# The causal mask of self-attention's diagonal blocks: a GpSimd select behind the exponential, or a TensorE product in front of it

## The chip, the cores and the metric

The kernel runs on one core of a Trainium2 chip. The metric is the device time of one launch in microseconds, lower is better. A core has five engines that run their own instruction streams and wait for one another by semaphores: TensorE (PE in the profile; its weight loads are listed apart as PEld), VectorE (DVE), ScalarE (ACT), GpSimd (POOL) and SyncE (SP), which here only issues DMAs.

## The reference, cut to what matters

One decoder layer: self-attention, cross-attention and a mixture of experts, each with a residual and a layer norm. The change touches self-attention alone, for 2 batches of 2048 tokens, 512 channels, 16 heads of 32:

```python
q = (x @ Wq.T + bq).reshape(B, T, H, D); k = ...; v = ...
scores = jnp.einsum('bqhd,bkhd->bhqk', q, k) * attn_scale[0]
masked = (qb >= kb) & (idx[None, :] - idx[:, None] - 2 * (kb - qb) >= 1)   # qb, kb: starts of 64-token chunks
scores = jnp.where(masked[None, None], -jnp.inf, scores)
attn = jax.nn.softmax(scores, axis=-1)
out = jnp.einsum('bhqk,bkhd->bqhd', attn, v).reshape(B, T, C)
return out @ Wo.T + bo
```

With i and j the places of key and query in their chunks of 64, this masks all keys of earlier chunks, in the query's own chunk those with i > j, and none of later chunks. The kernel computes the blocks of keys from a query's own block of 128 to the end of the sequence. In a diagonal block of 128 keys by 128 queries, the keys of the first chunk are masked for all queries of the second, the keys of the second chunk for none of the first, and within a chunk the keys that come after their query.

## The kernel before, in words

`self_attention` goes over 8 **groups** (2 batches, 4 groups of 4 heads). In a group the 2048 queries are cut into 4 chunks c of 512 (chunk 0 is the last 512 queries), and the keys into blocks of 128. A **round** is one chunk with one key block: `round_at` lists 40 rounds of a group, 4, 8, 12 and 16 for c = 0, 1, 2, 3; k numbers the rounds within a chunk, from the last key block down. The last four rounds of every chunk are those where the key block meets the chunk's own queries. There only `width` columns are left (512, 384, 256, 128 in the four), and the last 128 of them are the diagonal block. So 16 of 40 rounds are **diagonal rounds**. Two rounds make a **pair**, numbered 0 to 19 here; the diagonal pairs are 0 and 1 (c = 0), 4 and 5 (c = 1), 10 and 11 (c = 2), 18 and 19 (c = 3), the first of each two with 512 and 384 columns, the second with 256 and 128.

For one head of a round:

- TensorE writes the scores, 128 keys by `width` queries, into one of three PSUM banks `sbank` (L440). The rows of `kparts` and `qparts` carry high and low parts and the negated row maximum, so that a score comes out with its maximum already taken off. In a diagonal round a second product (L443), the bf16 identity `identb` by the bf16 `maskT`, adds -1e30 on the masked places, in the same bank.
- ScalarE takes the exponential from the bank into `probs` (L548), a ring of four rounds. `exp_done` tells of it; TensorE waits for the exponential of three heads before when it writes the next score.
- One pair later TensorE multiplies `probs` with the values (L458, `weighted`) and with ones for the denominator (L469). For the latter GpSimd first adds the pair's two rounds of `probs` into `both` (`add_pair`: a copy at L331 where the even round is wider, then the sum at L334), which takes 128 x 2048 elements in a full pair.

Around the scores, in the same TensorE stream, lie the **maxima segments** (L406): score products of a later chunk, on which VectorE takes row maxima (L607 with `maskS`, L611 without), through three banks `wbank`; the projections of keys, queries and values for a later chunk (L382, L389), whose results ScalarE (L513) and VectorE (L579, L591) take out and SP spreads over partitions by 12 DMAs a chunk (L227); and four transposes (L413) that bring the maxima into `qparts`, which ScalarE copies (L521). `maxima_in` and `others_in` say in which round each of them stands. In a pair's last round four segments are held back and stand between the products of `weighted`. At the start of a group's c = 0, VectorE also copies the last chunk's denominator (L645) and takes its reciprocal (L650), GpSimd multiplies (`multiply`, L344), and SP stores (L234) before it goes on to the next 12 spreading DMAs.

The order on every engine is the order of the code. TensorE's is: scores of pair p with their segments, then `weighted` of pair p - 1. ScalarE may start the exponentials of pair p when the products with pair p - 2 have read `probs` and GpSimd's sum of pair p - 2 is done.

## Time and profile before

| | |
|---|---|
| runs | 3275.59, 3286.88, 3287.71 us; median 3286.88 |
| the profiled execution | 3281.05 us, its span 3279.3 us |
| busy over the span | PE 2963.8 us (90%), DVE 2039.8 (62%), ACT 1453.1 (44%), POOL 1520.5 (46%) |
| self-attention | from 58 us (first score) to 1699 us, some 208 us for each of 8 groups |
| L443, the mask's product | 512 times in the program: 16 rounds x 4 heads x 8 groups |
| mean granted clock of TensorE | 0.961 of full |

The page lists, for each engine and line, how often a group of instructions ran, how long one took, and how long the engine was idle before it and on whom it waited. The timeline lists instructions with start and duration; like ones in a row are merged. Matmuls are pipelined: each is shown from its start to a modelled end, so how much of the engine one takes is read from the distance between two starts, and not from its duration.

### The profile page before, as it was taken

To read this page: it belongs to the slowest core of one execution; us is meant where nothing else is said; L and a number is where in the kernel's file an instruction comes from. 1 tells how busy PE (TensorE), PEld (TensorE's weight loads), DVE (VectorE), ACT (ScalarE), POOL (GpSimd) and SP (SyncE) were. 2 spreads that over 40 slices of the span, in tenths; PEclk is the share of its full clock that TensorE was granted. 3 is DMA by queue.
4 is the path that set the end of the run, shared out by engine and by line. 5 is a ranking of instruction groups with operands and counts; after the bars stand their busy time and mean duration, and the time that the engine had idled before them with its cause. 6 is when DMAs were issued, how large, how long until landed. Compare 5 with 4: busy or idle time off the path is not lost. (4 is left out here: it accounts for less than half of the span.)

```text
span 3279.3 us, 59175 instructions
## 1 busy us (share of the span) xinstructions
PE 2963.8 (90%) x19197; PEld 1934.0 (59%) x19197; DVE 2039.8 (62%) x4795; ACT 1453.1 (44%) x3375; POOL 1520.5 (46%) x1093
## 2 busy tenths in 40 slices
PE   7998999989989999898988979999799994999992
PEld 4444444444444444444434468888688883888882
DVE  4645646556465574554725568888477774777776
ACT  1443544434444444444442257777322222555551
POOL 3343443424434344243452234444377774665656
PEclk8999999999999999999999989999999996999996
DMA  4223022221221212212207522222222224999997
GB/s 114 62 64 82 7 74 79 58 63 32 75 78 44 66 44 74 78 31 67 66 30 253 189 84 88 79 82 84 84 71 68 68 61 140 258 254 259 257 254 265
DMA packets 185030, 343.33 MB, mean 105 GB/s; under 512 B 36136, under 2 KB 54696, under 8 KB 183848
## 3 DMA queue, kind: packets, MB, share of 16 engines
q1 hardware_dynamic: 135336, 250.90, 25.7%
q0 software_dynamic: 28800, 48.43, 6.8%
q10 hardware_dynamic: 20736, 41.95, 3.3%
q8 instruction: 92, 1.51, 0.2%
q14 instruction: 66, 0.54, 0.1%
HBM read 206.96 MB, written 83.89 MB: 89 GB/s over the span
## 5 line engine op out<-in xcount | busy, mean ns | idle before, releaser
L548 ACT ACTIVATE sa_probs<-sa_s 128x512 f32<-128x512 f32 (+3 forms) x1280 | 609.8, 540 | 692.9 <-PE sa_s L440 353.1
L334 POOL TENSOR_TENSOR sa_both<-sa_probs 128x2048 f32<-128x2048 f32 (+2 forms) x160 | 590.0, 3687 | 628.4 <-ACT sa_probs L548 616.9
L406 PE MATMUL sa_w<-sa_parts 96*128 96x512 f32 (+3 forms) x1280 | 515.0, 440 | 81.7 <-DVE sa_pmax L607 43.2
L440 PE MATMUL sa_s<-sa_parts 128*128 128x512 f32 (+3 forms) x1280 | 480.4, 409 | 27.3 <-ACT sa_probs L548 21.4
L607 DVE CUSTOM_DVE_ANT_0 sa_w<-sa_w,sa_maskS 128x512 f32<-128x512 f32 (+3 forms) x512 | 327.5, 649 | 238.7 <-PE sa_w L406 234.2
L406 PEld LDWEIGHTS sa_w<-sa_parts 96*128 96x128 f32 x1280 | 232.3, 195 | 409.4 <-issue 202.5
L611 DVE TENSOR_REDUCE sa_pmax<-sa_w 128x1 f32<-128x512 f32 (+3 forms) x768 | 422.7, 585 | 47.1 <-PE sa_w L406 44.0
L440 PEld LDWEIGHTS sa_s<-sa_parts 128*128 128x128 f32 x1280 | 242.0, 193 | 168.1 <-ACT sa_probs L548 96.6
L1519 POOL DMA_INDIRECT token_and_weight_of_slot<-rt_entry,rt_sl x256 | 261.0, 1020 | 124.4 <-issue 91.3
L458 PE MATMUL sa_pv<-sa_probs,sa_values 128*32 128x512 f32 (+3 forms) x2560 | 284.2, 538 | 0.0
L1252 ACT ACTIVATE xa_sm<-xa_sm,xa_nmax 128x154 f32<-128x154 f32 x512 | 209.4, 414 | 54.9 <-DVE xa_nmax L1175 54.9
L1831 POOL DMA_INDIRECT scratch_residual<-ex_y,ex_target x90 | 162.1, 1801 | 140.8 <-DMA scratch_residual<-ex_y,ex_target 109.2
L331 POOL COPY sa_both<-sa_probs 128x512 f32<-128x512 f32 x64 | 39.1, 611 | 342.7 <-ACT sa_probs L548 333.3
L1011 POOL TENSOR_TENSOR xa_pmain<-xa_sm,xa_rrec 128x2048 f32<-128x2048 f32 x32 | 115.9, 3622 | 109.8 <-DVE xa_rrec L1179 109.8
L469 PE MATMUL sa_pv<-sa_both,sa_ones 128*32 128x512 f32 (+1 forms) x1280 | 155.0, 556 | 0.0
L1893 PE MATMUL ex_yps<-ex_w2h,ex_hTh 128*128 128x512 f32 x540 | 148.1, 412 | 4.6 <-ACT ex_hTh L1926 4.3
L1876 PE MATMUL ex_h<-ex_xeT,ex_w1h 128*128 128x256 f32 x1080 | 145.4, 284 | 2.4 <-ACT ex_w1h L1905 2.4
L1041 PE MATMUL xa_qps<-cross_xT,cross_wq 128*128 128x128 f32 x1024 | 128.9, 281 | 20.4 <-DMA cross_xT<-scratch_x_T 16.2
L1876 PE MATMUL ex_h<-ex_xeT,ex_w3h 128*128 128x256 f32 x1080 | 145.3, 283 | 0.0
L1876 PEld LDWEIGHTS ex_h<-ex_xeT,ex_w1h 128*128 128x128 f32 x1080 | 139.7, 190 | 6.7 <-issue 2.8
L1876 PEld LDWEIGHTS ex_h<-ex_xeT,ex_w3h 128*128 128x128 f32 x1080 | 136.8, 190 | 0.0
L1041 PEld LDWEIGHTS xa_qps<-cross_xT,cross_wq 128*128 128x128 f32 x1024 | 123.1, 197 | 21.3 <-issue 21.3
(236 smaller groups left out, 5360.0 us busy)
## 6 DMA issues: line engine op xcount, KB each, us to landing
list_w<-in_w SPq DMA_DIRECT2D x138, 512.0 KB, 5.6
sa_parts<-early_halves SPq DMA_DIRECT2D x384, 128.0 KB, 2.4
early_xt<-in_xT SPq DMA_DIRECT2D x32, 1024.0 KB, 5.7
scratch_attention_T<-sa_oT SPq DMA_DIRECT2D x32, 256.0 KB, 2.4
on_at<-scratch_attention_T SPq DMA_DIRECT2D x32, 256.0 KB, 3.1
on_xr<-in_x SPq DMA_DIRECT2D x32, 256.0 KB, 3.4
scratch_x<-on_xn ACTq DMA_DIRECT2D x32, 256.0 KB, 2.1
scratch_x_T<-on_xnT ACTq DMA_DIRECT2D x32, 256.0 KB, 3.4
```

The source lines that it names most:

```text
L334: pool.tensor_tensor(both[:, p % 2, :, 0:w], probs[:, even, :, 0:w], probs[:, odd, :, 0:w], ALU.add).then_inc(both_ready, 1)
L406: nc.tensor.matmul(ps[:, 0:w], qparts[0:3 * HD, h, q0:q0 + P], kparts[0:3 * HD, h, k0:k0 + w], start=True, stop=True).then_inc(work_ready, 1)
L440: mm = nc.tensor.matmul(ps[:, 0:w], kparts[:, h, kb * P:(kb + 1) * P], qparts[:, h, q0:q0 + w], start=True, stop=not diag)
L458: mm = nc.tensor.matmul(pvbank[0][a:a + HD, 0:w], values[:, kb, h, :], probs[:, r % NPB, h, 0:w], start=kb == NKB - 1, stop=kb == QB * chu ...
L548: nc.scalar.activation(probs[:, r % NPB, h, 0:w], sbank[n % NSB][:, 0:w], ACT.Exp).then_inc(exp_done, 1)
L607: dve.tensor_tensor_reduce(out=wbank[b][:, 0:width_], in0=wbank[b][:, 0:width_], in1=maskS[:, 0:width_], scale=1.0, scalar=LOWEST, op0=ALU ...
L611: dve.tensor_reduce(pmax[:, j * GH + h, s:s + 1], wbank[b][:, 0:width_], AX.X, ALU.max).then_inc(work_free[b], 1)
L1041: mm = nc.tensor.matmul(qps[:, g * P:(g + 1) * P], wq[:, k, g * P:(g + 1) * P], xT[:, s, k], start=k == 0, stop=k == KT - 1)
L1252: nc.scalar.activation(sm[:, s, h], sm[:, s, h], ACT.Exp, bias=nmax[:, s, h:h + 1], accum_out=rsum[:, s, h:h + 1]).then_inc(exp_done, 1)
L1519: pool.indirect_dma_start(out=table, out_offset=bass.IndirectOffsetOnAxis(ap=sl[:, s, k:k + 1], axis=0), in_=entry[:, s, k], in_offset=Non ...
L1831: pool.indirect_dma_start(out=res, out_offset=bass.IndirectOffsetOnAxis(ap=target[:, s, j:j + 1], axis=0), in_=y[:, s, j], in_offset=None, ...
L1876: mm = nc.tensor.matmul(bank[f][:, 0:UNIT], wt[:, s, a, k, f * P:(f + 1) * P], xeT[:, s, b, k], start=k == 0 and n == 0, stop=k == KT - 1 ...
```

## The change

In diagonal rounds the product L443 is gone, with `identb` and `maskT`. The exponential is taken of unmasked scores. Behind it GpSimd runs `mask_round` in `add_pair`, before the copy and the sum of the pair: two selects in place on `probs` that write zero on masked places, the first on partitions 0 to 63 with 4 heads x 128 columns, the second on partitions 64 to 127 with 4 heads x 64 columns, each waited for by the next. `weighted` waits for the new semaphore `masked` in diagonal rounds, in place of `exp_done`. In the preparation on GpSimd three memsets and three selects fall away. `maskS` and the maxima stay.

```diff
+    diagonal = [r for r, (c, k) in enumerate(round_at) if kbs(c)[k] < QB * (chunk_q(c) + 1)]
+    NDIAG = len(diagonal)
+    MPARTS = 2
...
-            for t in (identb, identf, maskS, maskT, mcol):
+            for t in (identf, maskS, mcol):
                 step(pool.memset(t[:], 0.0))
...
+            def mask_round(it, r):
+                c, k = round_at[r]
+                w = width(c, kbs(c)[k])
+                pool.wait_ge(exp_done, it * NU + (NSB + GH * (r + 1)))
+                apart(pool, passed)
+                H = P // 2
+                done = (it * NDIAG + diagonal.index(r)) * MPARTS
+                pool.wait_ge(both_ready, it * NPAIR + (r // 2 + 2))
+                first = probs[0:H, r % NPB, :, w - P:w]
+                pool.affine_select(out=first, in_=first, compare_op=ALU.is_ge, fill=0.0, base=0,
+                                   pattern=[[0, GH], [-H, 2], [1, H]], channel_multiplier=-1).then_inc(masked, 1)
+                pool.wait_ge(masked, done + 1)
+                second = probs[H:P, r % NPB, :, w - H:w]
+                pool.affine_select(out=second, in_=second, compare_op=ALU.is_ge, fill=0.0, base=0,
+                                   pattern=[[0, GH], [1, H]], channel_multiplier=-1).then_inc(masked, 1)
+                pool.wait_ge(masked, done + 2)
+
             def add_pair(it, p):
                 even, odd = 2 * p % NPB, (2 * p + 1) % NPB
+                for r in (2 * p, 2 * p + 1):
+                    if r in diagonal:
+                        mask_round(it, r)
...
-                diag = kb < QB * (chunk_q(c) + 1)
                 mm = nc.tensor.matmul(ps[:, 0:w], kparts[:, h, kb * P:(kb + 1) * P], qparts[:, h, q0:q0 + w],
-                                      start=True, stop=not diag)
-                if diag:
-                    mm = nc.tensor.matmul(ps[:, w - P:w], identb[:], maskT[:], start=False, stop=True)
+                                      start=True, stop=True)
                 mm.then_inc(s_ready, 1)
...
-                    pe.wait_ge(exp_done, it * NU + (NSB + GH * r + GH))
+                    if r in diagonal:
+                        pe.wait_ge(masked, (it * NDIAG + (diagonal.index(r) + 1)) * MPARTS)
+                    else:
+                        pe.wait_ge(exp_done, it * NU + (NSB + GH * r + GH))
```

On TensorE, in the scores of pair 4 (c = 1, round of 512 columns going over into the round of 384), before. `sa_work_free` is VectorE's release of a bank of segments, `sa_exp_done` ScalarE's exponential:

```order
L406 MATMUL sa_w<-sa_parts 128x512 [waits sa_work_free2]
L440 MATMUL sa_s<-sa_parts 128x512 [waits sa_exp_done]
L443 MATMUL sa_s<-sa_maskT,sa_identb 128x128
L406 MATMUL sa_w<-sa_parts 128x512 [waits sa_work_free0]
L440 MATMUL sa_s<-sa_parts 128x384 [waits sa_exp_done]
L443 MATMUL sa_s<-sa_maskT,sa_identb 128x128
L406 MATMUL sa_w<-sa_parts 128x128 [waits sa_work_free1]
```

The same place in the changed kernel, where L425 is the segment's line and L458 the score's:

```order
L425 MATMUL sa_w<-sa_parts 128x512 [waits sa_work_free2]
L458 MATMUL sa_s<-sa_parts 128x512 [waits sa_exp_done]
L425 MATMUL sa_w<-sa_parts 128x512 [waits sa_work_free0]
L458 MATMUL sa_s<-sa_parts 128x384 [waits sa_exp_done]
L425 MATMUL sa_w<-sa_parts 128x128 [waits sa_work_free1]
```

The product between a score and the next segment or score is gone, nothing else moved there.

On GpSimd, the sum of pair 9 and the two diagonal pairs 10 and 11 (c = 2), before:

```order
L334 TENSOR_TENSOR sa_both<-sa_probs 128x2048 [waits sa_ones_done,sa_exp_done] x4
L331 COPY sa_both<-sa_probs 128x4x128 [waits sa_ones_done,sa_exp_done]
L334 TENSOR_TENSOR sa_both<-sa_probs 128x4x384 [waits sa_rest_copied]
L331 COPY sa_both<-sa_probs 128x4x128 [waits sa_ones_done,sa_exp_done]
L334 TENSOR_TENSOR sa_both<-sa_probs 128x4x128 [waits sa_rest_copied]
```

And in the changed kernel, from the same sum to the end of pair 10 (L350 is the copy, L353 the sum):

```order
L353 TENSOR_TENSOR sa_both<-sa_probs 128x2048 [waits sa_ones_done,sa_exp_done] x4
L330 AFFINE_SELECT sa_probs<-sa_probs 64x4x128 [waits sa_exp_done,sa_both_ready]
L334 AFFINE_SELECT sa_probs<-sa_probs 64x4x64 [waits sa_masked]
L330 AFFINE_SELECT sa_probs<-sa_probs 64x4x128 [waits sa_masked,sa_exp_done,sa_both_ready]
L334 AFFINE_SELECT sa_probs<-sa_probs 64x4x64 [waits sa_masked]
L350 COPY sa_both<-sa_probs 128x4x128 [waits sa_exp_done,sa_masked,sa_ones_done]
L353 TENSOR_TENSOR sa_both<-sa_probs 128x4x384 [waits sa_rest_copied]
```

Four selects stand ahead of the copy and the sum of a diagonal pair; the first two wait for the even round's exponentials alone.

On TensorE, `weighted` of pair 4 behind the scores of pair 5, before:

```order
L458 MATMUL sa_pv<-sa_probs,sa_values 32x512 [waits sa_exp_done]
L458 MATMUL sa_pv<-sa_probs,sa_values 32x512 x3
L458 MATMUL sa_pv<-sa_probs,sa_values 32x384 [waits sa_exp_done]
L458 MATMUL sa_pv<-sa_probs,sa_values 32x384 x3
L469 MATMUL sa_pv<-sa_both,sa_ones 32x512 [waits sa_both_ready]
```

And in the changed kernel (L477 the products with the values, L488 those with ones):

```order
L477 MATMUL sa_pv<-sa_probs,sa_values 32x512 [waits sa_masked]
L477 MATMUL sa_pv<-sa_probs,sa_values 32x512 x3
L477 MATMUL sa_pv<-sa_probs,sa_values 32x384 [waits sa_masked]
L477 MATMUL sa_pv<-sa_probs,sa_values 32x384 x3
L488 MATMUL sa_pv<-sa_both,sa_ones 32x512 [waits sa_both_ready]
```

The products stand where they stood, and wait for GpSimd's selects where they waited for ScalarE.

## Rows read from the trace of the kernel before

**Rows 1.** Busy time by window (PE, PEld, DVE, ACT, POOL, granted clock), one group.

```profile
400.00:607.00 207.00, 192.67 (x1064) 96.05 (x1063) 118.05 (x262) 91.91 (x187) 83.64 (x32) 0.97 0.22 61
```

**Rows 2.** Line L443: count, ns min/median/max, first and last start.

```profile
L443 PE MATMUL sa_s<-sa_maskT,sa_identb x512: 229/230/330, 58.7 to 1695.0; 128*128 128x128 bf16 x171
```

**Rows 3.** TensorE's timeline (start, duration in us), a round without a mask.

```profile
437.84 0.34 PE L406 MATMUL sa_w<-sa_parts 96*128 96x384 f32 x1
438.01 0.39 PE L440 MATMUL sa_s<-sa_parts 128*128 128x512 f32 x1
438.25 0.34 PE L406 MATMUL sa_w<-sa_parts 96*128 96x384 f32 x1
```

**Rows 4.** TensorE's timeline, diagonal pair 18.

```profile
456.02 0.48 PE L406 MATMUL sa_w<-sa_parts 96*128 96x512 f32 x1
456.34 0.40 PE L440 MATMUL sa_s<-sa_parts 128*128 128x512 f32 x1
456.58 0.23 PE L443 MATMUL sa_s<-sa_maskT,sa_identb 128*128 128x128 bf16 x1
456.62 0.48 PE L406 MATMUL sa_w<-sa_parts 96*128 96x512 f32 x1
```

**Rows 5.** ScalarE's timeline: exponentials of pairs 18 and 11, then of an unmasked round.

```profile
456.33 3.84 ACT L548 ACTIVATE sa_probs<-sa_s 128x512 f32<-128x512 f32 x8 [0.68 <-PE sa_s L443]
...
600.31 2.27 ACT L548 ACTIVATE sa_probs<-sa_s 128x256 f32<-128x256 f32 x8 [4.12 <-PE sa_s L443]
...
445.74 2.06 ACT L548 ACTIVATE sa_probs<-sa_s 128x512 f32<-128x512 f32 x4 [3.60 <-PE sa_s L440]
```

**Rows 6.** Groups by form, 200 to 1600 us: busy us, mean ns | idle before.

```profile
L548 ACT ACTIVATE sa_probs<-sa_s 128x384 f32<-128x384 f32 x108 | 48.0, 493 | 10.8 <-PE sa_s L443 10.4
L548 ACT ACTIVATE sa_probs<-sa_s 128x256 f32<-128x256 f32 x108 | 38.3, 384 | 127.6 <-PE sa_s L443 94.8 <-POOL sa_both L334 31.3
L548 ACT ACTIVATE sa_probs<-sa_s 128x128 f32<-128x128 f32 x108 | 25.0, 277 | 39.5 <-PE sa_s L443 37.4
```

**Rows 7.** VectorE by window, the scores of pair 4.

```profile
538.20:545.20 7.00, 6.86 (x19) 1.00 0.38 131
```

**Rows 8.** Timeline across pairs 1 and 2: GpSimd, SP's queue, TensorE.

```profile
701.17 1.27 POOL L344 TENSOR_TENSOR sa_oT<-sa_raw,sa_rden 128x512 f32<-128x512 f32 x1 [4.55 <-DVE sa_rden L650]
...
703.06 7.68 SPq L227 DMA_DIRECT2D sa_parts<-early_halves  x12
...
713.12 0.73 PE L406 MATMUL sa_w<-sa_parts 96*128 96x512 f32 x2
```

**Rows 9.** GpSimd's timeline while it prepares, the selects there are.

```profile
24.86 0.29 POOL L305 TENSOR_SCALAR_AFFINE_SELECT sa_identf<-sa_identf 128x128 f32<-128x128 f32 x1
...
25.72 0.23 POOL L313 TENSOR_SCALAR_AFFINE_SELECT sa_maskS<-sa_maskS 64x64 f32<-64x64 f32 x1
26.10 0.23 POOL L316 TENSOR_SCALAR_AFFINE_SELECT sa_maskT<-sa_maskT 64x64 bf16<-64x64 bf16 x1
```

**Rows 10.** GpSimd's groups by form: other operations, busy us and mean ns.

```profile
L1488 POOL IOTA rt_spare_row<- 128x256 int32 x1 | 0.4, 357 | 0.1
L334 POOL TENSOR_TENSOR sa_both<-sa_probs 128x2048 f32<-128x2048 f32 x79 | 360.6, 4565 | 532.8 <-ACT sa_probs L548 532.8
L1808 POOL COPY ex_source<-ex_token 128x2 int32 x47 | 34.1, 726 | 14.0 <-issue 8.6 <-PE ex_tps L1862 5.4
```

**Rows 11.** Timelines of GpSimd and TensorE: the sum of pair 4 and its reader.

```profile
546.06 3.46 POOL L334 TENSOR_TENSOR sa_both<-sa_probs 128x1536 f32<-128x1536 f32 x1 [0.18 <-POOL sa_both L331]
...
552.96 1.04 PE L469 MATMUL sa_pv<-sa_both,sa_ones 128*32 128x512 f32 x8
```

**Rows 12.** TensorE's timeline: the values' projection in pair 1, and in pair 16.

```profile
703.52 5.38 PE L389 MATMUL sa_w<-sa_wraw,early_xt 128*128 128x128 f32 x32
...
657.65 3.73 PE L389 MATMUL sa_w<-sa_wraw,early_xt 128*128 128x128 f32 x32
```

**Rows 13.** Busy time by window (columns as in rows 1), pair 1: the granted clock.

```profile
700.50:706.50 6.00, 4.79 (x21) 4.51 (x22) 3.63 (x14) 0.77 (x2) 1.27 (x1) 0.50 0.45 119
```

More of the change, by code:

```diff
@@ L183, in self_attention @@
         shift_ready = sem("shift_ready")
-        s_ready = sem("s_ready"); exp_done = sem("exp_done"); pv_done = sem("pv_done")
+        s_ready = sem("s_ready"); exp_done = sem("exp_done"); masked = sem("masked"); pv_done = sem("pv_done")
         both_ready = sem("both_ready"); rest_copied = sem("rest_copied"); ones_done = sem("ones_done")
@@ L303, in _ @@
             step(pool.memset(kparts[3 * HD:3 * HD + 2].bitcast(F32), 1.0))
-            for t in (identb, identf):
+            for t in (identf,):
                 step(pool.affine_select(out=t[:], in_=t[:], compare_op=ALU.not_equal, fill=1.0, base=0,
@@ L308, in _ @@
             step(pool.memset(maskS[H:P, 0:H], NEG))
-            step(pool.memset(maskT[0:H, H:P], NEG))
             for a in (0, H):
@@ L314, in _ @@
                                         pattern=[[-1, H]], channel_multiplier=1))
-                v = maskT[a:a + H, a:a + H]
-                step(pool.affine_select(out=v, in_=v, compare_op=ALU.is_ge, fill=NEG, base=0,
-                                        pattern=[[1, H]], channel_multiplier=-1))
             pool.sem_inc(consts_set, 1)
             pool.sem_inc(both_ready, 2)
+            def mask_round(it, r):
[14 more added lines that the diff above has]
+                pool.wait_ge(masked, done + 2)
             def add_pair(it, p):
                 even, odd = 2 * p % NPB, (2 * p + 1) % NPB
+                for r in (2 * p, 2 * p + 1):
+                    if r in diagonal:
+                        mask_round(it, r)
                 c, k = round_at[2 * p]
```

2 lines of the change are left out of this document (removed).

## The prediction, made before the changed kernel ran

> **What bounds the kernel now.** I read the busy time of one group of self-attention first. TensorE is busy 192.67 of 207 us, and no other engine comes near: VectorE 118, ScalarE 92, GpSimd 84 [rows 1]. The reader is to see that work taken from TensorE can be worth time here, and that GpSimd has 123 us a group to spare. An average does not tell where the work falls, so next I went through the timeline of one group, pair by pair, and asked of each diagonal pair what its TensorE stream waits for. Only there does the change act.
>
> **What a product costs TensorE.** 512 of them ran [rows 2], 64 a group. The duration of 230 ns is a latency, not a price. Starts tell the price. Without a mask a segment of 384 columns holds the engine 0.17 us (437.84 to 438.01) and a score of 512 columns 0.24 (438.01 to 438.25) [rows 3]; a segment of 512 columns at the same pace would take 0.23, together 0.47. In a diagonal round the segment of 512 takes 0.32 (456.02 to 456.34), the score 0.24, and the product itself 0.04 (456.58 to 456.62), together 0.60 [rows 4]. So a product costs 0.04 of its own and about 0.08 in the instruction behind it, 0.12 us together. If all of this were on the path, the change would give 64 x 0.12 x 8 = 61 us. The Trainium skill (TensorE: Matmul & The Clock Gate, "Back-to-back issue gap") has 81 ns for a matmul of 128 columns in a stream of weight loads and matmuls; by that figure the most would be 41 us. The rows show more, because a short product does not cover the weight load of what follows, and I use the rows.
>
> **What of it is on the path,** pair by pair, in one group:
>
> - Pairs 18, 5 and 11 are bound by ScalarE: their eight exponentials run without a gap, 3.84 us in pair 18 and 2.27 in pair 11, and pair 5 is built like 11 [rows 5]. TensorE can be only three scores ahead. What a faster TensorE can give is what the exponentials' own pace leaves. Four of 512 columns back to back took 2.06 us at about 0.60 each, so they start 0.49 apart, about 0.12 less than one lasts [rows 5]; with the same 0.12 off the durations of the narrower ones [rows 6] the others start 0.37 (384 columns), 0.26 (256) and 0.16 (128) apart. I take 0.19 for the last, since a weight load and a wait stand between. Pair 18: 4 x 0.49 + 3 x 0.37 + 0.49 = 3.56, which is 0.28 less than 3.84. Pair 11: 4 x 0.26 + 3 x 0.19 + 0.28 = 1.89, 0.38 less than 2.27. The first exponential starts about 0.08 sooner, and behind the last score the last product is gone (0.12). That is 0.5 for pair 18 and, rounded down for the ring of three banks, 0.4 each for 5 and 11.
> - Pair 19 (256 and 128 columns) has four segments among its first four scores, and TensorE is the later one there: four products at 0.12, and its last four scores are bound like pair 5's. I take 0.5. Pair 10 (seven segments in its first round) is TensorE's too, but for two products that stand ahead of a wait for VectorE: 0.6. Pair 0 has two projections; of its eight products two stand between the keys' projection and a wait for VectorE's half of it: 0.5.
> - Pair 4 has 16 segments for VectorE, which is busy 6.86 of 7.00 us there [rows 7]. TensorE only waits longer for a bank. I take 0.2, for the last scores.
> - Pair 1 gives nothing. Ahead of pair 2, TensorE's first segment needs keys and queries that come by 12 DMAs. These stand on SP behind the store of the last group's output, which waits for GpSimd's multiplication (701.17 to 702.44), which waited for VectorE's reciprocal. The DMAs are issued from 703.06 to 710.74 and TensorE's segment starts at 713.12 [rows 8]. That chain starts at the end of the last pair's products, in pair 0, and all eight products of pair 1 lie beside it.
>
> The sum is 0.5 + 0.4 + 0.4 + 0.5 + 0.6 + 0.5 + 0.2 = 3.1 us a group, of 7.7 that the products cost, or 24.8 in eight groups. The preparation loses six GpSimd instructions, worth nothing: they run until 27 us, and the first score is at 58 [rows 2, 9].
>
> **What the selects cost GpSimd.** A select of 128 columns took 0.29 us, one of 64 columns 0.23: 0.06 us for 64 elements, so 0.94 ns an element in each partition on top of 0.17 us [rows 9]. Between two that wait for each other lie 0.15 us (25.72 + 0.23 to 26.10) [rows 9]. The new ones have patterns of two and three levels, which no select of the trace has; the nearest row is an iota over 256 elements with several levels, 0.357 us [rows 10], no dearer than 0.17 + 256 x 0.94 ns = 0.41. So 512 elements cost 0.65, 256 elements 0.41, with two gaps M = 1.36 us a round, 16 x 1.36 = 22 us a group on an engine with 123 to spare. From above, M is bounded by other rows: a fixed part of 0.73 as in the copy of two elements, and the sum's 4565 / 2048 = 2.23 ns an element [rows 10], 2 x 0.73 + 768 x 0.00223 + 0.30 = 3.5 us. From below by the two gaps and the two fixed parts, 0.66. I take 1.36, because the nearest row is the same operation.
>
> **Who waits for them.** The new wait stands ahead of `weighted`; behind it on TensorE is queued everything that follows, the next pair's scores first. But `weighted` of a pair runs behind the scores of the next one. The tightest place is the sum: in pair 4 it ends at 549.52, and TensorE's product with ones starts at 552.96 [rows 11], 3.44 us of cover, which shrinks to some 2.9 as pairs 4 and 5 get shorter. The sum now comes later by M, as the even round's selects run beside the odd round's exponentials (4 x 0.37 = 1.5 us). 1.36 fits into 2.9, and pair 10 is alike. Behind pair 0's sum GpSimd's multiplication is next, for which it now sits idle 4.55 us until VectorE's reciprocal is there [rows 8]; a sum that ends 1.36 later does not delay it. At the end of the last group no pair covers the selects: 1.3 us, once.
>
> So 24.8 - 1.3 = 23.5 us: the profiled execution, 3281.05 us around a span of 3279.3, would take 3257.5. It lies 5.8 below the median of the runs shown; against the median the sum says 3263, which I forecast. With the terms that I chose between (0.2 to 0.7 for pair 4, 0 to 0.3 for pair 1, a tenth or two for the others either way) the gain is 15 to 35, the time 3252 to 3272.
>
> **The rivals.**
>
> - **More of the price comes through.** If VectorE and ScalarE give way with TensorE, since they wait for it between pairs, six tenths to all of 61 us are gained: 3226 to 3250. For it speaks that ScalarE is idle 4.12 us ahead of pair 11 [rows 5]; against it, that it has no gap within.
> - **Next to nothing.** TensorE's clock is 0.50 of full over 6 us in pair 1 [rows 13], behind a stretch where it stands still for VectorE, that is 1.2 in place of 2.4 GHz. There the values' projection took 5.38 us; at the full clock, in pair 16, 3.73 [rows 12]. With less work TensorE stands still longer there and in the ScalarE-bound pairs. If each group has one more such stretch, it costs 1.65 x 8 = 13 us, and the gain is 10: 3277. For it speaks that the clock falls in the group already where TensorE idles.
> - **GpSimd becomes late.** If the selects are dear, M above 1.5 delays the sum by 2M - 1.5, and TensorE waits 2M - 1.5 - 2.9 in pairs 4 and 10 each. This eats the 3.1 us a group from M = 3.0 on. At the bound from rows, M = 3.5, it is 8 x (2 x 2.6 - 3.1) = 17 us more than before: 3304. At M = 4.0, 33 more: 3320. Against it speak the selects' rows, 0.94 ns an element where the bound takes 2.23. The Trainium skill (GPSIMD Engine Reference, "Elementwise — side-by-side cycle accounting") has 12 cycles an element for branching that depends on data, which speaks against a select on GpSimd; by this page, as an estimate at its 1.2 GHz, a round would take 8 us and the kernel some 160 us more. The slope of rows 9 is a tenth of it.
> - **The change does not do what it says.** The order of the changed kernel shows no product in the scores and four selects a diagonal pair, so I leave this out.
>
> **How the numbers follow.** My forecast has 0.55, more of the price 0.12, next to nothing 0.23, GpSimd late 0.10. About 0.5% (16 us) is what a measurement here can tell from no change. Faster by more than that is below 3270.5: nearly all of the forecast's case and all of the first rival, 0.63. Slower is above 3303, most of the last case, 0.08. Within, 0.29. The range from 3238 to 3280 leaves out the better part of the first rival's lower end and the last rival, under 2 in 10.
>
> **What the profile of the changed kernel would show.** The price: starts of segment and score 0.47 apart in pair 18's first round, if ScalarE lets them. The exponentials of pair 11 in about 1.9 us, those of pair 18 in 3.5. VectorE still without a gap in pair 4. In pair 1 TensorE waits for the DMAs longer by some 0.5 us. The selects of 512 elements at 0.65 us and of 256 at 0.41, and no TensorE wait that GpSimd ends. I would be wrong if the selects took over 1.5 us a piece, if the granted clock fell in new places, or if groups got shorter by more than 4.5 us.

## The result, and the profile after

The changed kernel takes 3306.99 us in the median of five runs (3300.33 to 3308.62). The kernel before took 3286.88 in the median of the five beside it (3275.59 to 3288.60). The ratio is 1.0068 with a 95% interval of 1.0048 to 1.0088. I had forecast 3263 us and at most 3280. It came out slower.

In the traces, self-attention ends at 1719.5 us, before at 1704.4 (counted to the end of GpSimd's last multiplication), so 15.1 us are lost there. The two profiled executions are 26.0 us apart (spans of 3279.3 and 3305.3), the medians 20.1. The rest lies in stages that the change does not touch: the experts took 490.8 us against 484.1. Over the traces of this study that stage lies between 480 and 491 us with the same code, so I read nothing into it.

The busy time, as line 1 of the page:

```profile
PE 2952.7 (89%) x18685; PEld 1920.8 (58%) x18685; DVE 2068.2 (63%) x4795; ACT 1446.7 (44%) x3375; POOL 1656.9 (50%) x1343
```

TensorE lost 11 us of work, GpSimd took on 136, and **VectorE is 28 us busier, though the change gives it nothing to do**. One group by window (PE, PEld, DVE, ACT, POOL, granted clock), to set beside [rows 1]:

```profile
474.95:684.42 209.47, 191.45 (x1010) 93.79 (x1008) 121.66 (x262) 92.22 (x188) 100.92 (x65) 0.98 0.22 60
```

VectorE has the same 262 instructions and is busy 121.66 us, where it was 118.05. The selects are as forecast, by GpSimd's groups by form, 200 to 1600 us:

```profile
L353 POOL TENSOR_TENSOR sa_both<-sa_probs 128x1536 f32<-128x1536 f32 x26 | 90.0, 3462 | 4.8 <-POOL sa_both L350 4.8
L330 POOL TENSOR_SCALAR_AFFINE_SELECT sa_probs<-sa_probs 64x512 f32<-64x512 f32 x106 | 70.4, 664 | 169.9 <-ACT sa_probs L567 165.4 <-POOL sa_probs L334 3.6
L334 POOL TENSOR_SCALAR_AFFINE_SELECT sa_probs<-sa_probs 64x256 f32<-64x256 f32 x106 | 44.2, 417 | 7.2
```

**Which pairs changed.** I took the start of each pair's first score from the traces. The lengths at the full clock, in us; pairs not shown are the same:

| pair | before | product out, no selects | changed kernel |
|---|---|---|---|
| 0 | 14.46 | 14.20 | 14.20 |
| 4 | 9.48 | 9.37 | 9.37 |
| 5 | 5.73 | 5.53 | **6.66** |
| 10 | 9.01 | 8.54 | 8.55 |
| 11 | 5.40 | 5.19 | **6.32** |
| 18 | 8.42 | 8.04 | 8.04 |
| 19 | 7.10 | 6.95 | 6.95 |

Of these seven, five got shorter with the change and two longer. (Pair 1, which hangs on DMAs, varies between 16.6 and 18.2 us behind the first group in all three.) The engines in pair 5 of the third group, timelines of GpSimd, then VectorE, then TensorE (start, duration, what ended the idle time). L353 is the sum of pair 4 into `both`; L639 to L645 are `row_max`, which brings the row maxima of a chunk into shape for the transposes L432. L641 negates, L644 copies, L645 subtracts, 16 elements a partition each:

```profile
548.80 3.46 POOL L353 TENSOR_TENSOR sa_both<-sa_probs 128x1536 f32<-128x1536 f32 x1 [0.18 <-POOL sa_both L350]
552.33 0.69 POOL L330 TENSOR_SCALAR_AFFINE_SELECT sa_probs<-sa_probs 64x512 f32<-64x512 f32 x1
553.09 0.41 POOL L334 TENSOR_SCALAR_AFFINE_SELECT sa_probs<-sa_probs 64x256 f32<-64x256 f32 x1
```

```profile
550.01 0.20 DVE L639 TENSOR_REDUCE sa_mrow<-sa_pmax 128x16 f32<-128x48 f32 x1
550.25 2.04 DVE L641 TENSOR_SCALAR sa_mhi<-sa_mrow 128x16 fp32r<-128x16 f32 x1
552.32 0.18 DVE L644 COPY sa_mcol<-sa_mhi 128x16 f32<-128x16 f32 x1
552.41 0.65 DVE L645 SCALAR_TENSOR_TENSOR sa_mcol<-sa_mrow,sa_mhi 128x16 f32<-128x16 f32 x1
```

```profile
550.88 1.35 PE L458 MATMUL sa_s<-sa_parts 128*128 128x256 f32 x5 [0.32 <-ACT sa_probs L567]
553.20 0.63 PE L432 MATMUL sa_w<-sa_identf,sa_mcol 128*128 128x128 f32 x4 [0.97 <-DVE sa_mcol L645]
553.76 1.71 PE L477 MATMUL sa_pv<-sa_probs,sa_values 128*32 128x512 f32 x16
```

The negation of 16 elements "lasts" 2.04 us. It ends at 552.29, 0.03 behind the end of GpSimd's sum (552.26), and the subtraction ends at 553.06, 0.04 behind the end of the select. TensorE's transposes stand behind it and start 0.97 us late; all of `weighted`, and with it the next pair, is queued behind them. The same places of VectorE before:

```profile
548.62 0.20 DVE L620 TENSOR_REDUCE sa_mrow<-sa_pmax 128x16 f32<-128x48 f32 x1
548.85 0.69 DVE L622 TENSOR_SCALAR sa_mhi<-sa_mrow 128x16 fp32r<-128x16 f32 x1
549.66 0.18 DVE L626 SCALAR_TENSOR_TENSOR sa_mcol<-sa_mrow,sa_mhi 128x16 f32<-128x16 f32 x1
```

```profile
550.90 0.61 PE L413 MATMUL sa_w<-sa_identf,sa_mcol 128*128 128x128 f32 x4
```

There the negation starts at 548.85 and lasts 0.69: the sum ended at 549.52 [rows 11]. The subtraction ends at 549.84, and TensorE comes to its transposes only at 550.90, so this wait cost nothing. In all 16 places (pairs 5 and 11 of eight groups) the negation ends 0.03 us behind the sum, before and in the changed kernel alike. **The trace of before had the sign.** In pair 1, where nothing runs on GpSimd, the same instruction lasts 0.17. The sum was almost done when `row_max` came; the selects make it end 1.3 us later against VectorE, and that is what the negation has to wait for.

One more loss: in five places (pair 5 of three groups, pair 11 of two) the clock falls right behind this wait. Windows of the second group's pair 5, first the stretch ahead of the fall, in which the wait lies, then the one at the low clock:

```profile
340.00:343.20 3.20, 2.23 (x17) 1.36 (x20) 1.95 (x3) 1.86 (x8) 2.87 (x4) 1.00 0.00 0
343.20:346.60 3.40, 3.40 (x24) 0.74 (x16) 0.00 (x0) 1.90 (x4) 2.38 (x4) 0.50 0.02 5
```

The pair then takes 8.36 us in place of 6.66, so 1.7 us each.

### The profile page after: what moved, and what is told of

It is laid out like the page before. It is cut to its first block and busy times, and to the rows that moved or that the text cites. A ratio compares the mean times of both kernels' runs of the same rounds, so it can differ in the third digit from the quotient of the medians.

```text
span 3305.3 us, 58591 instructions
## 1 busy us (share of the span) xinstructions
PE 2952.7 (89%) x18685; PEld 1920.8 (58%) x18685; DVE 2068.2 (63%) x4795; ACT 1446.7 (44%) x3375; POOL 1656.9 (50%) x1343
## 5 line engine op out<-in xcount | busy, mean ns | idle before, releaser
L567 ACT ACTIVATE sa_probs<-sa_s 128x512 f32<-128x512 f32 (+3 forms) x1280 | 602.8, 541 | 693.1 <-PE sa_s L458 681.4
L353 POOL TENSOR_TENSOR sa_both<-sa_probs 128x2048 f32<-128x2048 f32 (+2 forms) x160 | 589.7, 3686 | 608.9 <-ACT sa_probs L567 596.8
L425 PE MATMUL sa_w<-sa_parts 96*128 96x512 f32 (+3 forms) x1280 | 504.3, 432 | 89.3 <-DVE sa_pmax L626 47.4
L458 PE MATMUL sa_s<-sa_parts 128*128 128x512 f32 (+3 forms) x1280 | 470.9, 406 | 34.9 <-ACT sa_probs L567 31.0
L425 PEld LDWEIGHTS sa_w<-sa_parts 96*128 96x128 f32 x1280 | 231.4, 193 | 450.3 <-issue 202.7
L458 PEld LDWEIGHTS sa_s<-sa_parts 128*128 128x128 f32 x1280 | 235.7, 191 | 191.1 <-ACT sa_probs L567 114.0
L477 PE MATMUL sa_pv<-sa_probs,sa_values 128*32 128x512 f32 (+3 forms) x2560 | 290.6, 548 | 0.8 <-POOL sa_probs L334 0.8
L330 POOL TENSOR_SCALAR_AFFINE_SELECT sa_probs<-sa_probs 64x512 f32<-64x512 f32 x128 | 85.1, 665 | 229.6 <-ACT sa_probs L567 223.5
L488 PE MATMUL sa_pv<-sa_both,sa_ones 128*32 128x512 f32 (+1 forms) x1280 | 158.0, 566 | 1.8 <-POOL sa_both L353 1.8
```

Of the source, the lines that this page charges most:

```text
L353: pool.tensor_tensor(both[:, p % 2, :, 0:w], probs[:, even, :, 0:w], probs[:, odd, :, 0:w], ALU.add).then_inc(both_ready, 1)
L425: nc.tensor.matmul(ps[:, 0:w], qparts[0:3 * HD, h, q0:q0 + P], kparts[0:3 * HD, h, k0:k0 + w], start=True, stop=True).then_inc(work_ready, 1)
L458: mm = nc.tensor.matmul(ps[:, 0:w], kparts[:, h, kb * P:(kb + 1) * P], qparts[:, h, q0:q0 + w], start=True, stop=True)
L477: mm = nc.tensor.matmul(pvbank[0][a:a + HD, 0:w], values[:, kb, h, :], probs[:, r % NPB, h, 0:w], start=kb == NKB - 1, stop=kb == QB * chu ...
L567: nc.scalar.activation(probs[:, r % NPB, h, 0:w], sbank[n % NSB][:, 0:w], ACT.Exp).then_inc(exp_done, 1)
```

## The experiments

The theory: **VectorE's small operations in `row_max` cannot run beside a GpSimd instruction; the selects push GpSimd's sum into their way.** The rivals: the selects hold up TensorE by themselves, through its wait for `masked`; or the removed products matter through TensorE's clock. The kernel before, run beside these, had medians of 3279.87 (experiments 1 to 4), 3280.52 (5 to 8) and 3281.97 us (9 and 10). The changed kernel was not run again beside them, so I compare with it by the ratios to before, 1.0068 for the changed kernel, and by the pairs.

**1. The product out, no selects** (`no_mask`; self-attention is left without its causal mask in the diagonal blocks):

```diff
-                if diag:
-                    mm = nc.tensor.matmul(ps[:, w - P:w], identb[:], maskT[:], start=False, stop=True)
```

> The mask's product is left out on TensorE and no select stands in its place, so the diagonal blocks are not masked. Theory: what was lost is GpSimd's sum of pairs 4 and 10, later by 1.36 us, which holds up VectorE's negation of the maxima; without selects the sum ends when it did, and the product's removal gives what the sum of the prediction said, 15 to 35 us less than before. In pairs 5 and 11 the negation still waits for the end of the sum, a few tenths longer than before, since TensorE comes sooner; pair 5 takes 5.4 to 5.8 us. Rival: the product was nearly free for TensorE, and the time is within 8 us of before.

3282.44 us, ratio 1.0011 [0.9998, 1.0024]. The whole is no measure here: other attention sends tokens to other experts, and the experts' last product then runs 552 times in place of 540, which makes that stage 493.7 us. By the whole the rival would be right, that gave it within 8 us of before. Self-attention alone ends 10.2 us sooner than before, 1694.2; that too is less than the 15 to 35 expected. Its pairs are the third column of the table: 0.26 + 0.11 + 0.20 + 0.47 + 0.21 + 0.38 + 0.15 = 1.78 us a group. So the product is worth about half of the 3.1 that I had taken, and the selects cost the changed kernel 25 us of self-attention. Of the 14.2 in eight groups, 5.1 are lost again, as the clock falls in three pairs 0 (15.9 us each in place of 14.2).

**2. Both masks**: the kernel before, with the selects besides.

```diff
+                for r in (2 * p, 2 * p + 1):
+                    if r in diagonal:
+                        mask_round(it, r)
...
+                    if r in diagonal:
+                        pe.wait_ge(masked, (it * NDIAG + (diagonal.index(r) + 1)) * MPARTS)
```

> The kernel before with its product kept and the selects added behind the exponential, so the blocks are masked twice. Theory: the selects alone cost what the changed kernel lost plus what the removal gave: in pairs 5 and 11 the negation lasts 2.0 us in place of 0.7 and 0.6, these pairs take 1.0 to 1.4 us more each, and where TensorE's clock falls there another 1.7; 20 to 45 us more than before in all. Rival (the selects are covered, and the changed kernel is slower for another reason, as unmasked exponentials or another order of the clock): within 8 us of before.

3306.79 us, ratio 1.0075 [1.0050, 1.0099]. Pair 5 takes 6.65 us where it took 5.73, pair 11 6.19 where it took 5.40, and three pairs 5 fell to the low clock (8.35). At the full clock no other pair differs, but for the last one (below, the tail); in pair 2 the clock fell in five groups where it fell in two before. The selects alone do the damage, products or not.

**3. The changed kernel with `row_max` in reductions.** Reductions of VectorE never got longer beside GpSimd in either trace, so the negation, copy and subtraction become reductions too (over one element, with negation, and a sum of two):

```diff
-                dve.tensor_reduce(mrow[:], pmax[:, :, 0:c + 1], AX.X, ALU.max).then_inc(mstep, 1)
...
-                dve.tensor_scalar(mhi[:], mrow[:], -1.0, None, ALU.mult).then_inc(mstep, 1)
+                dve.tensor_reduce(mpair[:, :, 0], pmax[:, :, 0:c + 1], AX.X, ALU.max, negate=True).then_inc(mstep, 1)
+                dve.tensor_reduce(mhi[:], pmax[:, :, 0:c + 1], AX.X, ALU.max, negate=True).then_inc(mstep, 1)
...
-                dve.tensor_copy(mcol[:, :, :, 0], hi32).then_inc(mstep, 1)
-                dve.scalar_tensor_tensor(out=mcol[:, :, :, 1], in0=mrow[:].rearrange("p (j h) -> p j h", j=QB),
-                                         scalar=-1.0, in1=hi32, op0=ALU.mult, op1=ALU.subtract).then_inc(mcol_ready, 1)
+                dve.tensor_reduce(mcol[:, :, :, 0], hi32, AX.X, ALU.max).then_inc(mstep, 1)
+                dve.tensor_reduce(mpair[:, :, 1], mhi[:].bitcast(F32).unsqueeze(2), AX.X, ALU.max, negate=True).then_inc(mstep, 1)
+                dve.tensor_reduce(mcol[:, :, :, 1], mpair[:].rearrange("p (j h) n -> p j h n", j=QB), AX.X, ALU.add).then_inc(mcol_ready, 1)
```

> The changed kernel, with VectorE's four operations behind the row maxima (reduction, negation by a constant, copy, subtraction of two tensors) written as five reductions of one SBUF tensor each. Theory: a reduction does not wait for GpSimd, so none of them lasts over 0.3 us, the transposes come as soon as the scores are done, pair 5 takes 5.0 to 5.5 us and pair 11 4.8 to 5.3, and the total is 20 to 45 us below the changed kernel, 5 to 25 below before. Rival (TensorE is late in pairs 5 and 11 for the selects themselves, or VectorE waits whatever it runs): within 8 us of the changed kernel, about 20 above before.

3278.87 us, ratio 1.0001 [0.9987, 1.0015]: the whole loss is gone. VectorE's and GpSimd's timelines at the same place as above:

```profile
548.95 0.20 DVE L639 TENSOR_REDUCE sa_mpair<-sa_pmax 128x16 f32<-128x48 f32 x1
549.07 0.19 DVE L640 TENSOR_REDUCE sa_mhi<-sa_pmax 128x16 fp32r<-128x48 f32 x1
549.29 0.18 DVE L643 TENSOR_REDUCE sa_mcol<-sa_mhi 128x16 f32<-128x16 f32 x1
549.38 0.16 DVE L644 TENSOR_REDUCE sa_mpair<-sa_mhi 128x16 f32<-128x16 f32 x1
549.58 0.19 DVE L646 TENSOR_REDUCE sa_mcol<-sa_mpair 128x16 f32<-128x32 f32 x1
```

```profile
547.73 3.46 POOL L353 TENSOR_TENSOR sa_both<-sa_probs 128x1536 f32<-128x1536 f32 x1 [0.18 <-POOL sa_both L350]
```

All five run under the sum, none over 0.22 us, and pairs 5 and 11 last 5.52 and 5.19 as without selects. Against the kernel before nothing is won, where 5 to 25 us were expected and 1.78 us a group should be. Self-attention ends 1.0 us sooner, of 14.2: in five of the seven pairs 0 behind the first group the clock fell (1.7 us each, 8.5), and the tail takes 3.8. That clock is the question of experiments 7 to 10.

**4. The kernel before with the same reductions**, no other edit, to see what they are worth by themselves:

> The kernel before, with the same five reductions. Theory: there too the negation waited, 0.5 us in pair 5 and 0.4 in pair 11, but the scores of these pairs hid it; 0 to 8 us less than before. Rival (the reductions themselves are faster or slower by some other way): over 10 us off before either way.

3279.01 us, ratio 0.9992 [0.9978, 1.0007]. Nothing, as the negation of before waited only while TensorE was still at its scores.

**5. Only the negation as a reduction.** The copy stays as in the changed kernel, and the subtraction too but for a sign, since `mrow` is now written negated; one of VectorE's waits between the two falls away:

```diff
-                dve.tensor_reduce(mrow[:], pmax[:, :, 0:c + 1], AX.X, ALU.max).then_inc(mstep, 1)
-                dve.wait_ge(mstep, i * (3 * NC) + (3 * c + 1))
-                dve.tensor_scalar(mhi[:], mrow[:], -1.0, None, ALU.mult).then_inc(mstep, 1)
+                dve.tensor_reduce(mrow[:], pmax[:, :, 0:c + 1], AX.X, ALU.max, negate=True).then_inc(mstep, 1)
+                dve.tensor_reduce(mhi[:], pmax[:, :, 0:c + 1], AX.X, ALU.max, negate=True).then_inc(mstep, 1)
...
-                                         scalar=-1.0, in1=hi32, op0=ALU.mult, op1=ALU.subtract).then_inc(mcol_ready, 1)
+                                         scalar=1.0, in1=hi32, op0=ALU.mult, op1=ALU.subtract).then_inc(mcol_ready, 1)
```

> The changed kernel, with VectorE's negation of the maxima alone written as a second reduction; the copy and the subtraction of two SBUF tensors behind it stay as they were. Theory (GpSimd holds an interface that VectorE needs for a one-input operation by a constant and for a second SBUF tensor alike): the wait only moves, the subtraction now lasts 1.5 to 2.0 us in pairs 5 and 11 where the negation did, pair 5 and pair 11 stay within 0.4 us of the changed kernel, and the total within 8 us of it. Rival (only the negation by a constant waits for the sum): the subtraction takes 0.2 to 0.7 us, the two pairs are 0.7 to 1 us shorter, and the total is 15 to 30 us below the changed kernel.

3284.65 us, ratio 1.0008 [0.9994, 1.0022]. The numbers are about the rival's (the subtraction 0.17 us, the two pairs 0.69 and 0.68 shorter, the total 20 us less by the ratios), but its mechanism is not what happened, and the theory named the wrong operation. The wait went to the copy, and the subtraction then ran at once. VectorE in the third group's pair 5, and GpSimd:

```profile
543.79 0.19 DVE L640 TENSOR_REDUCE sa_mhi<-sa_pmax 128x16 fp32r<-128x48 f32 x1
544.01 1.91 DVE L643 COPY sa_mcol<-sa_mhi 128x16 f32<-128x16 f32 x1
545.83 0.17 DVE L644 SCALAR_TENSOR_TENSOR sa_mcol<-sa_mrow,sa_mhi 128x16 f32<-128x16 f32 x1
```

```profile
542.44 3.44 POOL L353 TENSOR_TENSOR sa_both<-sa_probs 128x1536 f32<-128x1536 f32 x1 [0.19 <-POOL sa_both L350]
545.96 0.66 POOL L330 TENSOR_SCALAR_AFFINE_SELECT sa_probs<-sa_probs 64x512 f32<-64x512 f32 x1
```

The copy ends with the sum (545.92 and 545.88), and the subtraction gets in ahead of the select at 545.96. In the changed kernel the negation ended with the sum, the copy behind it slipped into the gap of 0.07 us, and the subtraction met the select. Here the pairs are 0.69 and 0.68 us shorter (6.66 to 5.97, 6.32 to 5.64): 0.48 is the subtraction's second wait (0.65 to 0.17), the rest is that one operation less is left behind the sum. With the shorter wait the clock fell in none of the pairs 5 and 11. The two waits are one mechanism; what decides is which of the three small operations finds GpSimd between two instructions.

**6. The sum in four instructions**, one a head, with `row_max` as in the changed kernel:

```diff
+                if wide > w and w > P:
+                    for h in range(GH):
+                        part = pool.tensor_tensor(both[:, p % 2, h, 0:w], probs[:, even, h, 0:w], probs[:, odd, h, 0:w], ALU.add)
+                    part.then_inc(both_ready, 1)
```

> The changed kernel, with GpSimd's sum of the pairs of 512 and 384 columns (0, 4, 10, 18) issued as four instructions, one a head, of about 1.0 us each. Theory (VectorE waits for the end of the GpSimd instruction that runs, and no longer): the negation lasts at most 1.1 us in pairs 5 and 11, in place of 2.0, with as much again possible for the subtraction behind it; the two pairs are 0.2 to 1.0 us shorter, the total 5 to 25 us below the changed kernel. Rival (it waits for GpSimd to be idle): the negation lasts 2.0 us and more, the sum being longer by about 0.5, and the total is 0 to 15 above the changed kernel.

3282.10 us, ratio 1.0004 [0.9991, 1.0017]. VectorE's and GpSimd's timelines, third group:

```profile
546.63 0.53 DVE L646 TENSOR_SCALAR sa_mhi<-sa_mrow 128x16 fp32r<-128x16 f32 x1
547.19 0.93 DVE L649 COPY sa_mcol<-sa_mhi 128x16 f32<-128x16 f32 x1
548.03 0.17 DVE L650 SCALAR_TENSOR_TENSOR sa_mcol<-sa_mrow,sa_mhi 128x16 f32<-128x16 f32 x1
```

```profile
545.16 3.90 POOL L355 TENSOR_TENSOR sa_both<-sa_probs 128x384 f32<-128x384 f32 x4 [0.18 <-POOL sa_both L350]
```

GpSimd does the same work and starts it at the same place, but each of the four instructions lasts about 0.98 us. VectorE's operations end at about 547.16, 548.12 and 548.20, so the first two wait for the end of the running one and no longer. It is the instruction that is waited for, not GpSimd's work. Pair 5 lasts 5.52 (5.81 in the first group). In pair 11 the subtraction met one more instruction in five groups (1.05 us), and the pair lasts 5.99 there, else 5.19 to 5.46.

**7 and 8. The chain in pair 1, with and without the change.** The forecast said that pair 1 hangs on the spreading DMAs, which stand behind the store of the last chunk [rows 8]. To give TensorE's saving a place where it could count, I moved reciprocal, multiplication and store of the last chunk into pair 1, with the store behind the next DMAs. VectorE's `normalize` moves with GpSimd's `multiply`, and the first line below stands behind the spreading DMAs. Once in the kernel before, once in the changed kernel with the five reductions:

```diff
+                if it > 0:
+                    store(it - 1, 3)
...
-                store(it, 3)
+                if not more:
+                    store(it, 3)
...
-                if p == 0 and behind is not None:
-                    multiply(behind[0], NC - 1)
+                if p == 1 and it > 0:
+                    multiply(it - 1, NC - 1)
```

> The kernel before, with VectorE's reciprocal of the last chunk, GpSimd's multiplication and the store of it moved from pair 0 of the next group to pair 1, and the spreading DMAs of chunk 2 issued ahead of that store. Theory: TensorE's stand of 4.1 us in pair 1 goes, with the low clock behind it, and the wait for the DMAs shrinks; pair 1 takes 10 to 13 us in place of 17, pair 2 18.5, and the total is 30 to 60 us below before. Rival (the DMAs' own way from the queries' low half sets the end of pair 1): pair 1 takes 14 us and more, and the total is under 25 us below before.

> The changed kernel with the five reductions and the same moves. Theory (the removed product's 1.8 us a group come through where the clock stays up, and were taken back in pairs 0 to 2 by it): 8 to 20 us below the kernel before with the same moves, no low clock in pairs 0 and 1. Rival (what the product gives is lost in another way, as a wait in pairs 0 to 2 for the same DMAs): within 6 us of it.

3239.96 us, ratio 0.9877 [0.9858, 0.9895], and 3238.09, ratio 0.9872 [0.9853, 0.9890]. Both beat both kernels of this case by over 1.2%. Behind the first group, pair 1 falls from between 16.7 and 17.9 us to 11.4 in the one and 11.1 to 12.2 in the other. The queue of SP and GpSimd in the first of the two, to set beside [rows 8]:

```profile
479.89 8.43 SPq L227 DMA_DIRECT2D sa_parts<-early_halves  x12
492.53 0.34 SPq L234 DMA_DIRECT2D scratch_attention_T<-sa_oT  x1
```

```profile
491.17 1.27 POOL L347 TENSOR_TENSOR sa_oT<-sa_raw,sa_rden 128x512 f32<-128x512 f32 x1 [0.94 <-DVE sa_rden L653]
```

The DMAs leave in the first microsecond of pair 1 instead of behind the multiplication. But the change itself again brings only 1.9 us where I had expected 8 to 20, the rival's size for a cause that it did not name. Self-attention ends 3.1 us sooner, of 14.2. The tail takes 3.8, and the traces show what took most of the rest. Windows over pair 0 of the third group, first the kernel without the change, then with it:

```profile
468.60:471.60 3.00, 3.00 (x11) 1.46 (x10) 0.00 (x0) 0.20 (x1) 0.00 (x0) 1.00 0.00 0
471.60:475.00 3.40, 2.47 (x12) 1.44 (x12) 2.74 (x8) 1.92 (x5) 0.00 (x0) 1.00 0.00 0
475.00:479.80 4.80, 4.80 (x34) 2.07 (x32) 0.94 (x3) 1.58 (x3) 4.06 (x2) 1.00 0.01 2
```

```profile
471.00:474.00 3.00, 3.00 (x11) 1.47 (x9) 0.00 (x0) 0.32 (x1) 0.77 (x2) 1.00 0.00 0
474.00:477.20 3.20, 1.84 (x8) 1.03 (x7) 2.54 (x6) 1.62 (x4) 0.00 (x0) 1.00 0.01 3
477.20:480.60 3.40, 3.40 (x6) 1.38 (x5) 0.48 (x3) 0.49 (x1) 2.27 (x4) 0.50 0.00 0
```

In the round that waits for VectorE's half of the keys, TensorE was busy 2.47 of 3.40 us with the products and 1.84 of 3.20 without, and then the clock is at half for 3.4 us. It falls on the queries' projection, eight products of 512 columns. Pair 0 takes 15.9 to 16.1 us in place of 14.2, in three of the seven groups behind the first; with the products it falls in none of these. That is 5.1 us; the first group, with more low clock in its pairs 0 and 2, loses 3. Between 60 and 1640 us the record of the granted clock has 10 stretches at half (34 us) with the change and 5 (17 us) without.

**9 and 10. Idle TensorE time filled again.** If this is so, a useless product that costs nothing on the path should help. The kernel of experiment 8, with one more product for each score of rounds 0 and 1, into the same bank, written over by the score; once 128 columns, once as wide as the score:

```diff
                 ps = sbank[n % NSB]
+                if r < 2:
+                    nc.tensor.matmul(ps[:, 0:P], kparts[:, h, kb * P:(kb + 1) * P], qparts[:, h, q0:q0 + P],
+                                     start=True, stop=True)
                 mm = nc.tensor.matmul(ps[:, 0:w], kparts[:, h, kb * P:(kb + 1) * P], qparts[:, h, q0:q0 + w],
```

> This is the changed kernel with the five reductions and the later end of the last chunk (3238.1 us, ratio 0.987), with one more product put on TensorE for each score of rounds 0 and 1 (pair 0): the first 128 columns of the same score, into the same bank, which the score then writes over. Theory 1 (it is TensorE's lower activity in pair 0, without the mask's product, that lets the clock be lowered there): pair 0 lasts 14.2 to 14.7 us in every group where it was 15.2 to 16.1 in 4 of 8, the low-clock time of self-attention falls from 78 to about 55 us, the group's mean length from 202.6 to 201.6 to 202.3 us, and the whole to about 3228 to 3236 us. Theory 2 (where the clock falls has nothing to do with the product; it falls in one place or the other): pair 0 is low in 2 to 5 groups as now, each product costs up to 0.12 us, 8 in a group, and the whole is 3238 to 3246 us.

> The same, with the added product as wide as the score (512 columns, some 0.2 us of TensorE each, 8 in a group). Theory 1: no low clock in pair 0, pair 0 at 14.5 to 15.3 us in every group (8 times up to 0.1 us more on the chain from score to exponential), so about 3230 to 3240 us. Theory 2: pair 0 low in 2 to 5 groups as now, and the whole 3240 to 3250 us.

3232.65 us, ratio 0.9841 [0.9819, 0.9862], and 3234.41, ratio 0.9855 [0.9839, 0.9872]. TensorE in pair 0 of the second group, first the kernel of experiment 8, then with the narrow product (L404 is the queries' projection):

```profile
271.09 0.38 PE L428 MATMUL sa_w<-sa_parts 96*128 96x256 f32 x1 [0.97 <-DVEq L605]
...
272.43 0.62 PE L461 MATMUL sa_s<-sa_parts 128*128 128x384 f32 x1
272.85 5.09 PE L404 MATMUL sa_w<-early_xt,sa_wq 128*128 128x512 f32 x8
```

```profile
269.26 0.39 PE L428 MATMUL sa_w<-sa_parts 96*128 96x256 f32 x1 [0.75 <-DVEq L608]
...
270.71 0.39 PE L464 MATMUL sa_s<-sa_parts 128*128 128x384 f32 x1
270.94 3.60 PE L404 MATMUL sa_w<-early_xt,sa_wq 128*128 128x512 f32 x8
```

The projection takes 3.60 us in place of 5.09. Pair 0 lasts 14.35 to 14.61 us in groups two to eight (14.48 to 14.70 with the wide product), and the stretches at half between 60 and 1640 us are 6 and 5 where they were 10. Only the first group's pair 0 still has one with the narrow product. The mean of groups two to seven is 201.7 us where it was 202.6; with the wide product it is 202.5, since pair 2 has 20 us of low clock in these groups (14 in experiment 8) and each pair 0 is 0.5 us longer than 14.20.

One trace of each kernel is little for a clock that falls here and there. But all twelve traces of this study say the same of pair 0. Behind the first group the clock falls there in 12 of 42 cases where pair 0 has no product beside its scores (0, 3, 5, 0, 1 and 3 of seven, in the changed kernel and experiments 1, 3, 5, 6 and 8), and in 1 of 42 with the mask's product or a useless one (in experiment 4). So the first theory of these two holds for pair 0, as a matter of how often: the changed kernel, without the products, has none there. For the whole, 5.4 us between the medians is what was expected, but the intervals of 0.9872 and 0.9841 overlap (0.9853 to 0.9862), and the wide product's (0.9839 to 0.9872) overlaps with both. So that the whole got faster is likely, and not shown.

## Why the prediction was wrong, point by point

- **"Who waits for them": the step that failed.** It asked only which TensorE product reads what GpSimd writes, found 3.44 us of cover for the sum of pair 4, and ended with "no TensorE wait that GpSimd ends". Except in the tail, that is true to the letter: the sum of pair 4 ends at 552.26 and its reader starts at 555.28. I had expected 2.9 - 1.36 = 1.5 us left between them; it is 3.0, because the reader itself comes late, and 1.9 in experiment 3 (551.19 to 553.08). But a GpSimd instruction has a second kind of waiter, VectorE's operations that cannot run beside it. They read nothing of the sum, no semaphore tells of them, and the profile books the wait as busy time. It costs 1.13 us a pair, twice a group (6.66 - 5.53, 6.32 - 5.19), 18 us in eight groups, and with it five stretches of low clock at 1.7, 8.5 us. Together 26.6. With the tail (below, 3.8 us) and less the 5.1 that the kernel without selects loses by three stretches of low clock in pair 0, that is the 25.3 us between the ends of self-attention in experiment 1 and in the changed kernel. It closes so exactly by chance: the first group's pair 0, 1.7 us longer in the changed kernel, and pairs 1 and 2 and rounding, as much shorter, cancel.
- The Trainium skill has this rule (SBUF — State Buffer, "Who interferes with whom"): a VectorE instruction in a two-port mode, which copies and operations by a constant can enter, or one with two inputs in SBUF against a GpSimd instruction that reads SBUF, shares ports with GpSimd; the one that is first has them for its whole instruction and the other waits, and on trn2 a reduction never contends. The traces agree where GpSimd is first: 2.04 us for the negation, 1.90 for the copy in experiment 5, 0.65 for the subtraction of two inputs, never over 0.22 for a reduction of `row_max`. No run here shows the other order. I had looked up what the selects cost and what speaks against a select, and not what else a busy GpSimd blocks.
- **"What of it is on the path": right in kind, too large.** 1.78 us a group came where the steps gave 3.1. Pair 18 gave 0.38 for 0.5, pair 5 0.20 and pair 11 0.21 for 0.4 each, pair 10 0.47 for 0.6, pair 0 0.26 for 0.5, pair 4 0.11 for 0.2, pair 19 0.15 for 0.5. In pairs 5, 11 and 18 the error is the exponentials' pace without the product: eight in 2.11 us where I had 1.89, and in 3.60 where I had 3.56; ScalarE still waits a little for TensorE. In pair 19 I had charged TensorE with four products of 0.12; how much of them ScalarE hid there I did not measure apart. The price of 0.12 holds, as two scores with a segment between them start 0.48 apart in pair 18 (669.42, 669.90), where segment, score and product took 0.60 before [rows 4]:

```profile
669.42 0.40 PE L458 MATMUL sa_s<-sa_parts 128*128 128x512 f32 x1
669.66 0.40 PE L425 MATMUL sa_w<-sa_parts 96*128 96x512 f32 x1
669.90 0.40 PE L458 MATMUL sa_s<-sa_parts 128*128 128x512 f32 x1
```

- **"What the selects cost": right.** 0.664 and 0.417 us where 0.65 and 0.41 were forecast, a round every 1.36 us (552.33 to 553.69). The rival of late selects, for TensorE's own wait, and that of a dear select both fall. The slope from the two selects of 64 and 128 columns [rows 9] carried to patterns of three levels.
- **The tail: too small.** I had 1.3 us. From the last pair's first score to the end of self-attention it is 15.4 us in the changed kernel, and 11.6 without selects. GpSimd and TensorE at the end of the last group:

```profile
1707.96 0.66 POOL L330 TENSOR_SCALAR_AFFINE_SELECT sa_probs<-sa_probs 64x512 f32<-64x512 f32 x1
...
1711.42 1.26 POOL L353 TENSOR_TENSOR sa_both<-sa_probs 128x512 f32<-128x512 f32 x1 [0.18 <-POOL sa_both L350]
```

```profile
1712.74 1.08 PE L488 MATMUL sa_pv<-sa_both,sa_ones 128*32 128x256 f32 x8 [1.82 <-POOL sa_both L353]
```

  The sum of pair 18 ends just before 1707.96, so both rounds' selects (2.67 us) stand between the two sums, and not one; the sum of pair 18 had itself come 1.4 us later behind the scores. Here TensorE does wait for GpSimd, 1.82 us, against the "no TensorE wait that GpSimd ends". And the clock is at half from 1711.9, so that the last eight products take 1.08 us, 0.61 in experiment 1.
- **Pair 1: right.** It took none of the gain. Experiments 7 and 8 show its chain by removing it: 40 us in eight groups.
- **The rival "next to nothing": it was the better forecast of the rest.** It took 13 us off for the clock and left a gain of 10. With VectorE's wait out of the way (experiment 3) the gain over before is 1.0 us, ratio 1.0001 [0.9987, 1.0015], nearer to that than to 23.5 and still short of it. That its 3277 stands so close to experiment 3's 3278.87 is luck: it was worked out from a kernel before at 3286.88. Experiments 8 to 10 show the clock at work. Its place was named wrongly: I had pair 1, which was at half clock before too, and it came in pair 0. Between 60 and 1640 us there are 12 stretches at half before and 15 in the changed kernel, 17 in experiment 3 and nine in experiment 4.
- **The range** went down to 3238 for more of the price and up only to 3280. The chance of slower, 0.08, came from dear selects alone.

What stays open: in which groups the clock falls. Five of sixteen waits of about the same length in pairs 5 and 11 brought a stretch of low clock, and eleven did not; in experiment 2 it was three of sixteen. TensorE's busy time ahead of it does not tell them apart: in the second group it was busy 2.23 of 3.20 us (340.00 to 343.20) and the clock fell, in the third 2.23 of 3.20 (551.40 to 554.60) and it stayed. Nor did I split the 1.5% of the last kernels further.

## What to carry to other kernels

Before work goes to an idle GpSimd, look at what VectorE runs beside it: each small copy, operation by a constant or operation with two inputs that has them all in SBUF waited here for the end of the GpSimd instruction that was running. Where the input came from PSUM it did not: the copy of a denominator, 128 x 512, always lasted 0.68 to 0.69 us in the changed kernel, and 16 of 31 lay wholly beside GpSimd's instructions. In the profile this shows as a duration, not as a wait, so compare the shortest and the longest duration of one line; 0.17 us against 0.56 to 0.95 in the kernel before, on a line that leads to the critical engine, was the warning. Reductions do not have this, and a long GpSimd instruction can be cut into several. And a product taken from TensorE near a place where it stands still can lose by the clock some of what it saves.

## What the runs showed of the hardware that I had not expected

- An operation of VectorE on 16 elements a partition, 0.17 us by itself, took 2.04 us beside a GpSimd sum and ended 0.03 us behind it. The same held for a copy (1.90) and an operation with two inputs (0.65 to 1.05). The reciprocal of 512 elements (3.29 to 3.35 us in all 31 cases, 24 of them at least in part beside GpSimd) and reductions kept their durations.
- A useless product in front of eight scores a group made the kernel no slower and probably faster: 3232.65 us (3222.72 to 3234.10) beside 3238.09 (3236.86 to 3238.91), with the queries' projection at 3.60 us in place of 5.09.
